# A four-stage Mamba and mixture-of-experts kernel: one normalization moves from GpSimd to ScalarE, and the loads for the first scans are issued together

## The reference

```python
x = x + _layernorm(_L0_attn_ref(_layernorm(x), ...))
# in _L0_attn_ref, with x already normalized:
xp = einsum('bld,de->ble', x, W_x)            # 64 columns dt_low, 16 B, 16 C
dt = softplus(dt_low @ W_dt + b_dt)
# per token t:  h = exp(dt_t * A) * h + (dt_t * x_t) * B_t ;  y_t = h . C_t
```

## Time and profile before

| | us |
|---|---|
| median of 3 runs | 3620.82 (3619.66 to 3627.6) |
| the profiled execution: its own time | 3620.82 |
| the profiled execution: span, first to last instruction | 3619.1 |
| PE busy | 3145.1 (87%) |
| DVE busy | 1859.7 (51%) |
| POOL busy | 1620.7 (45%) |
| ACT busy | 1376.2 (38%) |

### The profile page before, as it was taken

One profiled execution on the slowest core, in us unless ns is written; L12 is line 12 of the kernel. 1 busy time (PEld: TensorE's weight loads), 2 busy tenths in 40 slices (PEclk: granted clock), 3 DMA queues, 4 the chain that ended last, 5 costly groups with the idle time before them and its releaser, 6 DMA issues. The chain is left out here.

```text
span 3619.1 us, 45197 instructions
## 1 busy us (share of the span) xinstructions
PE 3145.1 (87%) x15190; PEld 2580.5 (71%) x15190; DVE 1859.7 (51%) x2762; ACT 1376.2 (38%) x2443; POOL 1620.7 (45%) x1491
## 2 busy tenths in 40 slices
PE   5455798998988996989999999999999999999950
PEld 3233577777777775888888888888888888888840
DVE  6698989989899971552232222222322222223238
ACT  5454676676666752311221312213213122131114
POOL 4187787887888873510421502304114033050025
PEclk8655799999999997979999999999999999999985
DMA  7859688696796845810311302203113022031039
GB/s 252 247 168 243 175 225 228 199 262 194 211 243 198 246 139 171 249 44 15 98 57 41 99 21 73 74 12 107 48 47 95 19 79 74 15 111 36 15 129 347
DMA packets 281673, 480.09 MB, mean 133 GB/s; under 512 B 30497, under 2 KB 106097, under 8 KB 281474
## 3 DMA queue, kind: packets, MB, share of 16 engines
q1 hardware_dynamic: 223104, 296.62, 28.2%
q0 software_dynamic: 56704, 180.38, 16.8%
q10 hardware_dynamic: 1666, 0.36, 0.1%
HBM read 380.18 MB, written 97.11 MB: 132 GB/s over the span
## 5 line engine op out<-in xcount | busy, mean ns | idle before, releaser
L1418 DVE CAST hh<-h 128x512 fp32r<-128x512 f32 (+1 forms) x400 | 156.8, 392 | 1295.5 <-ACT h L1270 1289.7
L1270 ACT ACTIVATE h<-c_psH,b1e 128x512 f32<-128x512 f32 (+1 forms) x384 | 237.9, 619 | 1348.7 <-PE c_psH L1589 1325.9
L817 POOL TENSOR_TENSOR u<-dtxs,Bt 128x512 f32<-128x512 f32 x512 | 665.2, 1329 | 164.2 <-DVE b_psA L721 147.2
L721 DVE TENSOR_TENSOR_SCAN b_psA<-b_psA,carry,u 128x512 f32<-128x512 f32 x512 | 656.3, 1282 | 60.3 <-ACT b_psA L594 55.5
L1338 POOL DMA_INDIRECT xrow<-xt_d,idx x80 | 90.2, 1128 | 1091.6 <-PE c_psT L1580 585.9
L1631 PE MATMUL c_psY<-W2h,hh 128*128 128x512 f32 x1344 | 533.4, 397 | 0.1
L925 PE MATMUL b_psY<-ident,pr 128*128 128x128 f32 x2048 | 349.8, 310 | 210.7 <-DVE pr L728 192.8
L1631 PE MATMUL c_psY<-W2h,hl 128*128 128x512 f32 x1344 | 525.3, 391 | 0.0
L1631 PE MATMUL c_psY<-W2l,hh 128*128 128x512 f32 x1344 | 524.6, 390 | 0.0
L925 PEld LDWEIGHTS b_psY<-ident,pr 128*128 128x128 f32 x2048 | 268.8, 158 | 296.2 <-DVE pr L728 243.8
L728 DVE TENSOR_TENSOR pr<-b_psA,Ct 128x512 f32<-128x512 f32 x512 | 354.0, 691 | 20.2 <-DMA Ct<-bc_d 2.5
(11 more groups left out here) (251 smaller groups left out, 5606.3 us busy)
## 6 DMA issues: line engine op xcount, KB each, us to landing
w<-ws_d POOLq DMA_DIRECT2D x224, 512.0 KB, 6.6
raw<-in_w SPq DMA_DIRECT2D x256, 256.0 KB, 2.7
Bt<-bc_d SPq DMA_DIRECT2D x64, 512.0 KB
Ct<-bc_d SPq DMA_DIRECT2D x64, 512.0 KB, 21.4
y_d<-yst SPq DMA_DIRECT2D x80, 256.0 KB
xn<-in_x SPq DMA_DIRECT2D x8, 1024.0 KB, 6.9
xT_d<-xnT SPq DMA_DIRECT2D x8, 1024.0 KB, 8.4
dt_d<-a_dt SPq DMA_DIRECT2D x8, 1024.0 KB, 7.5
```

What stands on the lines that cost most here:

```text
L721: nc.vector.tensor_tensor_scan(psA[q][:, :], psA[q][:, :], u[g % U_RING][:, :], carry[:, k:k + 1], ALU.mult, ALU.add).then_inc(s_h, 1)
L817: nc.gpsimd.tensor_tensor(u[g % U_RING][:, :], dtx[s % 2][:, :], Bt[n // TG][:, n % TG, :], ALU.mult)\
L1270: nc.scalar.activation(h32[:, 0:n * P], psH[j % 2][:, 0:n * P], ACT.Gelu, bias=b1[:, j - 1:j]).then_inc(s_gelu, 1)
```

## The change

The four normalizing instructions of each chunk leave GpSimd's list and become four ScalarE activations (Identity with a scale and a bias for each partition) in a new function `norm(c)`. Step i of ScalarE now is `evacuate(i-1)`, `norm(i)`, `decay(i-2)`, `project(i-1)`, `log(i-2)`. GpSimd keeps the small instructions. On SP the loads for the first scans are no longer spread over the steps: all 16 table loads and the 5 pass loads are issued together at the end of step 5. The number of DMAs and their sizes are the same.

```diff
--- before.py
+++ after.py
@@ -123,12 +123,11 @@
                 sp.wait_ge(s_dx, c + 1)
                 sp.dma_start(columns(dtx_d, c), dx[c % 2][:, :, :]).then_inc(s_odx[c % 2], 16)
 
-            def load_first_tables(j):
+            def load_first_scans():
                 sp.wait_ge(s_obc[0], 16)
-                load_table(sp, bc_d, early["Bt"], early["s_B"], 0, j, 0)
-                load_table(sp, bc_d, early["Ct"], early["s_C"], NS, j, 0)
-
-            def load_first_passes():
+                for j in range(NG):
+                    load_table(sp, bc_d, early["Bt"], early["s_B"], 0, j, 0)
+                    load_table(sp, bc_d, early["Ct"], early["s_C"], NS, j, 0)
                 sp.wait_ge(s_odt[0], 16)
                 sp.wait_ge(s_odx[0], 16)
                 sp.wait_ge(s_oxT[0], 16)
@@ -145,10 +144,8 @@
                     store_bc(i - 2)
                 if 0 <= i - 3 < NCH:
                     store_dt(i - 3)
-                if 0 <= i - 3 < NG:
-                    load_first_tables(i - 3)
-                if i == NCH + 1:
-                    load_first_passes()
+                if i == 5:
+                    load_first_scans()
             for c in range(NCH - 2, NCH):
                 sp.wait_ge(s_obc[c % 2], (c // 2 + 1) * 16)
                 sp.wait_ge(s_odt[c % 2], (c // 2 + 1) * 16)
@@ -177,11 +174,6 @@
                 pool.wait_ge(s_neg, c + 1)
                 pool.wait_ge(s_rs, c + 1)
                 nc.gpsimd.tensor_tensor(nmr[q][:, :], nmr[q][:, :], rstd[q][:, :], ALU.mult).then_inc(s_nm, 1)
-                pool.wait_ge(s_nm, c + 1)
-                a = xn[c % XR]
-                for t in range(CT):
-                    nc.gpsimd.tensor_scalar(a[:, t, :], a[:, t, :], rstd[q][:, t:t + 1], nmr[q][:, t:t + 1],
-                                            ALU.mult, ALU.add).then_inc(s_xn, 1)
 
         @block.scalar
         def _(act):
@@ -201,6 +193,13 @@
                     act.wait_ge(s_xT, c * DT + d + 1)
                     nc.scalar.copy(xnT[c % XR][:, d, :], psT[d % 2][:, :]).then_inc(s_xnT, 1)
 
+            def norm(c):
+                act.wait_ge(s_nm, c + 1)
+                a, q = xn[c % XR], c % 2
+                for t in range(CT):
+                    nc.scalar.activation(a[:, t, :], a[:, t, :], ACT.Identity, bias=nmr[q][:, t:t + 1],
+                                         scale=rstd[q][:, t:t + 1]).then_inc(s_xn, 1)
+
             def decay(c):
                 act.wait_ge(s_z, c + 1)
                 after(act, s_low, c)
@@ -222,6 +221,8 @@
             for i in steps(0, 3):
                 if 0 <= i - 1 < NCH:
                     evacuate(i - 1)
+                if 0 <= i < NCH:
+                    norm(i)
                 if 0 <= i - 2 < NCH:
                     decay(i - 2)
                 if 0 <= i - 1 < NCH:
```

## The result

| us | before | changed |
|---|---|---|
| median (lowest to highest), 4 runs each, same chip | 3622.31 (3619.66 to 3627.6) | 3646.23 (3643.51 to 3653.09) |
| the profiled execution: its own time, span | 3620.82, 3619.1 | 3653.11, 3651.4 |
| end of prepare, first instruction of mix on ScalarE | 173.84 | 198.99 |
| first `rs` activation of experts on ScalarE | 1414.98 | 1442.09 |

The ratio of the changed kernel to the one before is 1.0072, with a 95% interval of 1.0056 to 1.0088: it is slower, by 24 us between the medians. The forecast was 3641 us, in the range 3618 to 3659. The two profiled executions differ by more, 32.3 us: 25.15 in prepare, 1.96 in mix and about 5 in experts and combine. Only the first part lies where the kernels differ.

What follows compares the result with a forecast made beforehand. Prepare was taken as bound by a chain of waits through a_psZ, with SP's loads and stores served in order. ScalarE 0, wait behind the block 19.0 and clock 1 made +20 us: 3641 us, range 3618 to 3659.

Steps and rivals of the forecast that it cites:

- VectorE's relief: Prepare's rounds: without GpSimd normalizing, VectorE's correction ends sooner; at most 1.5 us gained, 1.2 taken.
- The tables' rate: Block at step 5: 8.39 MB of tables at 200 GB/s take 42.0 us, bounds 295 and 148 GB/s.
- the sum: Prepare: 0 for ScalarE, 19.0 us wait at chunk 6's copy and 1 for the clock make 20 us.
- divided by the share, since in a block no engine runs dry: Tables: window rates divided by DMA busy share give 295, 217, 180 and 233 GB/s.
- four undivided windows: Earlier trace of prepare, where a pair of tables moves: 224, 165, 148 and 168 GB/s.
- The start: Ahead of the block: data flows from 75.5, and 4.26 MB at 405 GB/s take 10.5 us, to 86.0.
- The passes' rate: Block's end: five pass and skip loads, 1.31 MB at 139 GB/s, take 9.4 us.
- The clock's term: Z matmuls after TensorE stood idle: 1 us added of a possible 2.2.
- The upper bound on record: Prepare: with tables at 148 GB/s taking 56.7 us, and 2.2 for the clock, +36 us.
- no wait at all: Rival, block at step 5: moves at 405 GB/s, store_bc(4) lands at 113.5, total 3619 us; chance 0.16.
- The queue sets the pace: Rival, SP's list: 16 tables at 3.43 us each, store_bc(4) lands at 148.0, total 3648 us; chance 0.15.
- ScalarE becomes the bound: Rival, ScalarE's gap in prepare closes: up to 3.2 us in up to 7 rounds, about 3663 us; chance 0.04.

Runs made afterwards that it cites:

- e2: Kernel before with only the 21 loads issued together at the end of step 5, normalization still on GpSimd: 3649.52 us, ratio 1.0073.
- e1: Kernel before with only the normalization moved to ScalarE, loads spread as before: 3623.37 us against 3626.32, ratio 0.9998.
- e4: Changed kernel with the five pass loads issued at step 9 as before the change: 3641.28 us, before 3624.90.
- e5: Changed kernel with the 16 table loads reading distinct contiguous rows of x instead of repeated bc_d rows: 3626.38 us, before 3626.32.
- e8: Changed kernel with each table load repeating two adjacent rows of x, 4 KB in one piece, for 128 partitions: 3625.59 us, before 3628.14.
- e9: Changed kernel with each table load reading 256 distinct rows of dt_d, 16 KB apart: 3624.24 us, before 3628.14.
- e11: Changed kernel, block included, with four DRAM tensors laid out chunk by chunk: 3602.21 us against 3628.14 before, ratio 0.9931.
- e3: Changed kernel with the 21 loads issued by GpSimd, passes first, stores staying on SP: 3640.54 us against 3624.90 before, ratio 1.0042.
- e7: Changed kernel with all stores issued from ScalarE's queue, SP issuing only loads: 3641.84 us against 3626.32 before, ratio 1.0049.

## Why the prediction was right, and which terms were off

The mechanism was as forecast: `store_bc(4)` behind the block, one wait of the seventh copy, the loop behind it late, mix untouched. e2 shows that it is the block, and e1 that the normalization on ScalarE costs nothing: it takes 2.93 us a chunk in a gap of which 2.34 stay.

**VectorE's relief is next to nothing.** The prediction took 1.2 us for it. Chunk 5's Abs does start 1.4 us sooner (115.51 against 116.94), but not for that reason. The rounds before it last 17.07 us (81.37 to 98.44) where they lasted 17.12 (81.00 to 98.12). L266 is shorter, as forecast, but TensorE now starts z straight behind its own transposes, and a shorter correction ahead of that buys 0.05 us a round. What differs at chunk 5 is the length of its z matmuls, in the kernel before, in the changed kernel and in e2, where GpSimd still normalizes:

```profile
109.75 7.15 PE L301 MATMUL a_psZ<-xpT,wdt 97*128 97x512 f32 x8 [0.34 <-DVE a_dt L250]
109.70 5.77 PE L302 MATMUL a_psZ<-xpT,wdt 97*128 97x512 f32 x8
110.31 5.48 PE L298 MATMUL a_psZ<-xpT,wdt 97*128 97x512 f32 x8 [0.32 <-DVE a_dt L247]
```

The granted clock from 110 to 117 us was 0.52 before, near the lower of the two levels, and 0.72 in the changed kernel; why it was lower there in that execution is not shown. e2 has the same Abs at 115.83, 1.1 us sooner than before, without any relief of VectorE. That the 1.2 us came out near the measured 1.4 is luck, and it did no harm, since the wait ate it either way.

**The tables' rate was mis-sized.** The windows of the changed kernel show the borders of the tables and of what comes behind them:

```profile
89.00:140.00 51.00, 24.05 (x64) 12.07 (x64) 24.60 (x19) 24.88 (x26) 1.66 (x4) 0.71 0.86 166
140.00:144.00 4.00, 0.00 (x0) 0.00 (x0) 0.00 (x0) 0.00 (x0) 0.00 (x0) 0.50 1.01 347
```

The tables take 51 us at 166 GB/s, where the sum had 42.0 at 200. The step "divided by the share, since in a block no engine runs dry" failed: inside the block the recorded share is only 0.86, though SP always had more to issue. Three of the four undivided windows, 148 to 168 GB/s, were the right reading; the fourth, 224, was not.

**The start was set too early.** The sum lets data flow from 75.5 and the stores be through at 86.0. The load of chunk 7 was issued at 75.61, but the engines moved 55 GB/s from 77 to 78 us and 397 from 78.5 on. With 10.5 us for the 4.26 MB that is 89.0, where the slow stretch begins.

**The passes' rate was off the other way.** The 1.31 MB fit into the 4 us from 140 to 144, where I took 9.4 from the window 155 to 161. That window still held a pair of tables, issued at 149.21 and 149.81, right ahead of the passes. (e4, a comparison of two executions, gave 5.3 us for them.) The three errors, +9.0, +3.0 and -5.4 us, make 6.6 of the 6.75 us by which the copy starts later than 140.9. That the third takes back nearly half of the other two is luck.

**The clock's term was net nothing.** Chunk 6's z took 5.85 us, 1.1 more than the earlier trace rows, as the term had it, but chunk 7's took 5.81 and not 6.96. From the copy to the end of prepare it was 0.55 us less than before; all but 0.06 of it lies behind chunk 7's Abs (22.08 against 22.57).

So 25.7 us late at the copy less 0.55 make the 25.15 of prepare, where the sum said 20; the medians differ by 23.9. The upper bound on record, +36 us, is 3657 and not the 3659 of the range.

Of the rivals, *no wait at all* is what e5, e8, e9 and e11 show once the source of the tables is another. The rule of the Trainium skill (DMA: Bandwidth & Descriptors, section "Anatomy of one DMA — SWDGE (gpsimd) path"), bytes by 436 GB/s, gives an estimate of 22 us for the block. That is near what e11 shows (its block is issued from 78.8 to 102.2) and 0.4 of the 55 us that the changed kernel shows. *The queue sets the pace* gave 148.0 for the landing and 3648 us in all, closer to the 147.5 and 3646 measured than my own 140.9 and 3641, and yet it was not the cause: tables of the same number and size hold SP 0.5 to 1.8 us each in e11. The issue time followed the drain. *ScalarE becomes the bound* needed the gap closed, and it did not close.

What is open: why repeated reads of two rows 16 KB apart are slow (the distance, or less likely the pieces of 2 KB), and where the recorded idle 0.14 of the DMA engines in the block comes from. Neither was tried further.

## What to carry to other kernels

Before moving a group of loads together, find the rate of exactly these loads in a window where they are nearly alone, and use it as it stands; then look for the first store behind them and the buffer it frees. If the same bytes are slow, ask how they lie in memory before asking when they are issued: here one changed layout gained 23 us, while issuing the loads together lost 24 and, with the new layout, nothing. A wait names the transfer that came late, not the one that made it late.

## What was not expected of the hardware

- Two 2 KB rows 16 KB apart, each read 128 times by one load, move at 165 GB/s; two rows in one 4 KB piece at 389 to 399 (e8, e11), 256 different rows with the same distance at 395 (e9), different rows in 4 KB pieces at 408 (e5).
- These slow loads harm transfers of other queues too: issued by GpSimd they still cost 14 us of prepare (187.51 against 173.84).
- An engine that issues a DMA behind such loads is held with no semaphore to wait for: SP up to 5.58 us for one table in the changed kernel and 23.35 us for one store of 64 KB in e3, ScalarE up to 7.71 us for one store of 1 MB in e7.
